# Projecting queries and keys for the next four heads inside the attention loop, one product block per head

## The reference

```python
qkv = x @ W_qkv.T + b_qkv
q, k, v = jnp.split(qkv, 3, axis=-1)          # b, l, 16 heads, 32
scores = jnp.einsum('bqhe,bkhe->bhqk', q, k) * scale
scores = jnp.where(causal[None, None], scores, -jnp.inf)
attn = jax.nn.softmax(scores, axis=-1)
out = jnp.einsum('bhqk,bkhe->bqhe', attn, v)
```

## Time and profile before

| | us |
|---|---|
| median of 3 runs | 1772.81 (1772.62 to 1774.22) |
| the profiled execution's own time | 1772.19 |
| its span in the profile | 1770.0 |
| TensorE busy | 1706.3 (96%) |
| VectorE busy | 1043.6 (59%) |
| ScalarE busy | 736.7 (42%) |
| GpSimd busy | 253.5 (14%) |
| first weights of the projections asked for | at 639.7 |
| first score matmul of the attention | at 784.8 |
| last exponential of the attention | at 1181.5 |

### The profile page before, as it was taken

How to read it: one execution, slowest core, us unless ns; L and a number is a source line. 1 busy time by engine, 2 the same in 40 slices (tenths; PEclk the granted TensorE clock), 3 DMA queues, 4 the chain that set the end, 5 groups by cost and what they waited for, 6 DMA issues and landing times. The chain is left out here.

```text
span 1770.0 us, 24385 instructions
## 1 busy us (share of the span) xinstructions
PE 1706.3 (96%) x8366; PEld 1374.3 (78%) x8366; DVE 1043.6 (59%) x1795; ACT 736.7 (42%) x1528; POOL 253.5 (14%) x247
## 2 busy tenths in 40 slices
PE   6999999999999979979999899999999999999998
PEld 4777878778788868867777677777888888888887
DVE  4322455465424453449999799984565554655776
ACT  4421322232213332239999899982222222222221
POOL 4001200200300030100000000005144031033230
PEclk9999999999999989989999999999999999999999
DMA  7200210110100137833445245505010010011243
GB/s 290 91 13 0 66 42 29 43 48 13 48 7 24 48 111 259 289 152 87 121 138 139 82 132 161 142 27 177 1 48 24 1 48 24 1 48 54 90 131 132
DMA packets 75670, 149.61 MB, mean 85 GB/s; under 512 B 9497, under 2 KB 26521, under 8 KB 74018
## 3 DMA queue, kind: packets, MB, share of 16 engines
q1 hardware_dynamic: 75554, 148.17, 26.9%
HBM read 101.87 MB, written 46.27 MB: 84 GB/s over the span
## 5 line engine op out<-in xcount | busy, mean ns | idle before, releaser
L1509 DVE TENSOR_TENSOR pt_lo<-p_turn,pt_hi 128x512 fp32r<-128x512 f32 (+3 forms) x384 | 201.0, 550 | 25.4 <-ACT pt_hi L1484 17.8
L1502 DVE TENSOR_REDUCE row_top<-p_score 128x1 f32<-128x128 f32 (+7 forms) x256 | 189.5, 750 | 20.9 <-PE p_score L1436 20.6
L1476 ACT ACTIVATE prob<-p_score,row_top 128x128 f32<-128x128 f32 (+7 forms) x256 | 189.8, 744 | 7.9 <-DVE row_top L1502 5.8
L1484 ACT ACTIVATE pt_hi<-p_turn 128x512 fp32r<-128x512 f32 (+3 forms) x384 | 182.0, 493 | 12.7 <-issue 4.9
L1447 PE MATMUL p_turn<-ident,prob 128*128 128x128 f32 x1152 | 183.4, 278 | 3.7 <-DVE pt_lo L1509 3.4
L958 DVE TENSOR_TENSOR hid<-hid,p_up 128x512 f32<-128x512 f32 x64 | 44.0, 688 | 222.3 <-PE p_up L435 206.6
L1845 DVE TENSOR_TENSOR e_hid<-e_hid,e_p_up 128x512 f32<-128x512 f32 x64 | 44.0, 687 | 196.7 <-PE e_p_up L1731 196.7
L1462 PE MATMUL p_o<-pt_hi,v 128*128 128x512 f32 (+3 forms) x384 | 149.2, 396 | 3.9 <-ACT o_both L1492 3.1
L1447 PEld LDWEIGHTS p_turn<-ident,prob 128*128 128x128 f32 x1152 | 133.4, 143 | 17.6 <-DVE pt_lo L1509 4.3
L1434 PE MATMUL p_score<-stack 128*128 128x512 f32 (+3 forms) x384 | 129.8, 393 | 13.9 <-PEq L53 7.0
L705 ACT ACTIVATE hid<-p_gate 128x512 f32<-128x512 f32 x64 | 38.3, 598 | 223.1 <-PE p_gate L435 223.0
(11 more groups left out here) (259 smaller groups left out, 4004.0 us busy)
## 6 DMA issues: line engine op xcount, KB each, us to landing
stack<-qk_parked SPq DMA_DIRECT2D x256, 128.0 KB, 3.9
raw<-in_wgu SPq DMA_DIRECT2D x64, 256.0 KB, 2.8
qk_parked<-qk SPq DMA_DIRECT2D x16, 1024.0 KB, 3.9
v_parked<-v_out SPq DMA_DIRECT2D x16, 512.0 KB, 5.3
v<-v_parked SPq DMA_DIRECT2D x8, 1024.0 KB, 9.4
o_parked<-o_both SPq DMA_DIRECT2D x64, 128.0 KB
res<-in_x SPq DMA_DIRECT2D x8, 512.0 KB
rot<-in_w2t SPq DMA_DIRECT2D x4, 1024.0 KB, 7.4
```

The lines of the kernel that those rows point to most:

```text
L1476: act.activation(prob[r // QB][:, h % 2, r % QB, 0:width_of(r)], p_score[:, r % 2, 0:width_of(r)], ACT.Exp, bias=top[:, r:r + 1], accum_ou ...
L1484: act.activation(pt_hi[:, (BL * h + j) % PT, c0:W], p_turn[:, (BL * h + j) % TB, c0:W], ACT.Copy).then_inc(rounded, 1)
L1502: dve.tensor_reduce(top[:, r:r + 1], p_score[:, r % 2, 0:width_of(r)], AX_X, ALU.max, negate=True).then_inc(topped, 1)
L1509: dve.tensor_tensor(pt_lo[:, slot, c0:W], p_turn[:, (BL * h + j) % TB, c0:W], pt_hi[:, slot, c0:W].bitcast(F32), ALU.subtract).then_inc(sp ...
```

## The change

`project_qkv` becomes `project_first`: it makes quad 0's 8 blocks and the 16 value blocks only. The loops over quads 1 to 3 are gone on all engines, and so is the second half of the values' load, which SP now issues at the start of the attention. SP's order changes too: mask and all 32 loads of the first two stacks come right behind the four stores of quad 0, ahead of the first value store.

The 24 other blocks are made in the attention. Head h of quads 0 to 2 gets the step `job`: four groups of three matmuls on TensorE, a copy on ScalarE, rounding and remainder on VectorE; SP stores every second block, and waits for that store to land before loading the stacks of the next quad. GpSimd splits the next quad's weights in the attention. The block takes a place in the ring of `p_turn`: 13 per head in place of 12, in quad 3 too, where no block is made. The waits that follow from it are in `turn`.

```diff
-                   ("weigh", 5, 0), ("score", 6, 1), ("turn", 11, 0), ("weigh", 6, 0), ("turn", 0, 1),
-                   ("score", 7, 1), ("weigh", 7, 0), ("turn", 1, 1), ("turn", 2, 1), ("weigh", 8, 0),
-                   ("score", 0, 2), ("weigh", 9, 0)],
+                   ("weigh", 5, 0), ("score", 6, 1), ("turn", 11, 0), ("weigh", 6, 0), ("job", 0, 0),
+                   ("turn", 0, 1), ("job", 1, 0), ("score", 7, 1), ("job", 2, 0), ("weigh", 7, 0), ("job", 3, 0),
+                   ("turn", 1, 1), ("weigh", 8, 0), ("score", 0, 2), ("turn", 2, 1), ("weigh", 9, 0)],
...
-                   ("round", 1, 1), ("exp", 7, 1)],
+                   ("job", 0, 0), ("round", 1, 1), ("exp", 7, 1)],
...
-                   ("top", 6, 1), ("rest", 10, 0), ("rest", 11, 0), ("top", 7, 1), ("rest", 0, 1)],
+                   ("top", 6, 1), ("rest", 10, 0), ("rest", 11, 0), ("top", 7, 1), ("rest", 0, 1),
+                   ("job", 0, 0)],
...
+        def slot_of(h, j):
+
+            return ((BL + 1) * h + j) % TB
...
-                wait(pe, split, BL * (HB * it + h) + j - TB + 1)
+                past = j - TB + 1 if j >= TB else (-1 if h and j == 0 else 0)
+                wait(pe, split, BL * (HB * it + h) + past)
+                if h == 0 and j == 1 or h and j == 2:
+                    used = HB * it + h
+                    wait(pe, job_used, min(used, HB * (QUADS - 1)) if isinstance(it, int) else used)
...
+            def job(it, h, k):
+                i, t = divmod(h, 4)
+                if isinstance(it, int) and it == QUADS - 1:
+                    return
+                if k == 0:
+                    if t == 0:
+                        pe.wait_ge(w_split[i], it + 1)
+                    pe.wait_ge(split, BL * (HB * it + h) + BL - TB + 1)
+                acc = p_turn[:, slot_of(h, BL)]
+                pe.matmul(acc, w_hi[:, i, k], x_hi[:, t, k], start=(k == 0), stop=False)
+                pe.matmul(acc, w_hi[:, i, k], x_lo[:, t, k], start=False, stop=False)
+                mm = pe.matmul(acc, w_lo[:, i, k], x_hi[:, t, k], start=False, stop=(k == KD - 1))
+                if k == KD - 1:
+                    mm.then_inc(job_done, 1)
...
+            def job_out(it, h, _):
...
+                act.wait_ge(job_done, HB * it + h + 1)
...
+                wait(act, qk_split, HB * it + h)
+                act.activation(val[:], p_turn[:, slot_of(h, BL)], ACT.Identity, bias=pair_bias[:, h // 4:h // 4 + 1],
+                               scale=scale[:, 0:1]).then_inc(job_used, 1)
...
+                dve.tensor_copy(hi, val[:]).then_inc(qk_rounded, 1)
+                dve.wait_ge(qk_rounded, HB * it + h + 1)
+                dve.tensor_tensor(lo, val[:], hi.bitcast(F32), ALU.subtract).then_inc(qk_split, 1)
...
+                    wait(pool, job_done, HB * (quad - 2) + 4 * i + 4 if quad > 1 else 0)
```

More of the change, by code:

```diff
@@ L1136, in _, with load_w @@
         def _(sp):
[L1137 to L1154, removed]
+            def load_w(i):
+                sp.dma_start(raw_w[:, i], wqk[0, i]).then_inc(w_loaded[i], 16)
+            load_w(0)
+            sp.dma_start(bias[:, 0:2 * QUADS], qk_bias).then_inc(consts, 16)
             sp.dma_start(scale[:], qk_scale).then_inc(consts, 16)
-            load_w(0, 1, True)
+            load_w(1)
             for k in range(KD):
                 sp.dma_start(raw_v[:, k], wv[:, k]).then_inc(wv_loaded, 16)
-            body(0, False)
+            for n in range(4):
+                sp.wait_ge(qk_split, 2 * n + 2)
+                sp.dma_start(qk_dram[2 * (n % 2) + n // 2].rearrange("h p n -> p h n"), qk[:, n % 2].bitcast(F32))\
+                    .then_inc(qk_stored[n % 2], 16)
+            sp.dma_start(mask_f[:], masks).then_inc(mask_loaded, 16)
+            for i in range(2):
+                sp.wait_ge(qk_stored[i], 32)
+            for n in range(2):
+                load_stack(sp, stack, qk_dram, 0, n, first_loaded)
             for m in range(NT):
@@ L1290, in _, with attention @@
             dve.tensor_copy(mask[:], mask_f[:])
-            with dve.Fori(1, QUADS) as it:
-                body(it, False)
-def attention(nc, mask, stack, v, ident, qk_dram, v_dram, o_dram, total, o_both, o_stored, load_next):
+def attention(nc, wqk, x_hi, x_lo, bias, scale, staging, mask, stack, v, ident, qk_dram, v_dram, o_dram, total, o_both, o_stored,
+              load_next):
     G = 2
@@ L1388, in _, with next_weights @@
         def _(sp):
+            def next_weights(quad):
+                for i in range(2):
+                    wait(sp, w_split[i], quad - 1)
+                    sp.dma_start(raw_w[:, i], wqk[quad, i]).then_inc(w_loaded[i], 16)
             def next_stack(it, n):
                 sp.wait_ge(scored, 2 * ROWS * (4 * it + n - 1))
+                wait(sp, qk_stored, 16 * (4 * (it - 1) + 2 * (n % 2) + n // 2 + 1) if it else 0)
                 load_stack(sp, stack, qk_dram, it, n, stacked[n % 2])
@@ L1402, in store_o @@
                     .then_inc(o_stored[(G * h + g) % OS], 16)
-            def body(it, first, last):
+            next_weights(1)
+            load_values(sp, v, v_dram, 0, 1, v_second)
+            for it in range(QUADS):
+                last = it == QUADS - 1
+                if last:
+                    sp.wait_ge(qk_stored, 16 * 4 * (QUADS - 1))
+                    load_next(sp)
                 for h in range(HB):
-                    for g in range(G):
-                        store_o(it, h, g)
+                    store_o(it, h, 0)
+                    if h % 2 and not last:
+                        store_job(it, h // 2)
+                    store_o(it, h, 1)
                     n = h // 2 + 2
@@ L1455, in weigh @@
                     wait(pe, v_loaded[b], 16 * it)
+                    if b == 1 and isinstance(it, int) and it == 0:
+                        pe.wait_ge(v_second, 16)
                 if kb == 0:
```

199 lines of the change are left out of this document (107 added, 92 removed).

## The result

The changed kernel takes 1819.95 us (median of 4 runs, 1819.19 to 1824.16), the kernel before beside it 1773.51 us: a ratio of 1.0265, 95% interval [1.0246, 1.0284]. The forecast was 1820. Ratios here compare undisturbed executions alone; the profiled one of the run e5_narrow_split took 2146 us, so it is left out and none of its rows is read. The profiled execution of the changed kernel took 1819.19 us with a span of 1817.2, against 1772.19 and 1770.0 before. The page's line of busy times says almost nothing about it: TensorE's share went from 96% to 95%.

The account below looks back on a forecast made before the run. Bound: paths through three engines at 93 to 98% of a 12.06 us head. Terms -55.0 + 90.0 + 7.4 + 2.9 + 5.0 = +50.3 us on 1772.2 gave 1822, stated as 1820; 8-in-10 range 1786 to 1834.

Parts of the forecast that it names:

- The removal and SP's queue: Start of attention: 65.7 us earlier without the 24 blocks, less 6.5 stall and 4.2 clock, leaves 55.0 us.
- The stall: Value phase: stack loads ahead delay the first value store, landing in 3.4 us, so TensorE's block 8 waits 6.5 us.
- The clock: TensorE after the gap near 691 us: granted clock of about a half, 4.2 us of work lost.
- Rival 3: Value phase: value stores do not stall TensorE; 10.7 us less, 1809 us; counted within the forecast's 0.58.
- A head with a product block: Seam of two heads: path of 5.94 us, 3.42 more, plus 0.32 on VectorE; 3.74 a head, 90 us for 24.
- The borders: At three borders of four heads turn 1 needs the block's copy finished, some 1 us each; 2.9 us.
- The collisions: Attention: GpSimd's splitting of weights meets VectorE's block split, four meetings of 1.8 us less what is hidden; 5 us.
- The stall in the loop's jump stays: Jump of the attention's loop: its stall remains, as the loops do; no change in time forecast.
- 1: Heads: TensorE alone is the limit, a head grows by 1.9 us, 46 in all; 1763 us, chance 0.10.
- 4: Heads: VectorE leads, its 1.07 us and collisions make a head grow by 4.5 us; 1838 us, chance 0.08.
- 5: Heads: waits of up to 1 us bring the lower clock, adding 34 us; 1854 us, chance 0.03.
- 2: Heads: unseen slack takes 1 to 1.5 us off the path of each of 24; 1784 to 1796 us, chance 0.19.

Follow-up runs that it names:

- e5_narrow_split: Changed kernel with VectorE's rounding and remainder of a product block over 8 of 512 columns in the loop's 16 heads; 1816.63 us, ratio 1.0234 to before.
- e4_last_ring: Changed kernel with 12 places of the ring per head in the last quad; 1812.75 us, ratio 1.0225 to before.
- e10_loads_later: Changed kernel with first weight stack loaded after the sixth value store, second stack and value load at the attention's start; 1808.46 us, ratio 1.0195 to before.
- e2: Changed kernel without the second group of three matmuls of each product block, between turn 0 and score 7; 1804.33 us, ratio 1.0169 to before.
- the new tables: Changed kernel with another order inside heads, split one head later, 12-place last ring, later loads, middle loop written out; 1754.49 us, ratio 0.9886 to before.

## Why the prediction was right, step by step

The time agrees to 0.05 us, which is luck: the sum gave 1822, and the 2 us taken off it as "a few tenths I counted twice" rest on no row; the terms were off by up to 3.4 us each, and most of the errors cancel. What holds up is the mechanism of the large term, the path through a head. The spans rose by 47.2 us: the first maximum of row 7 starts 54.5 us earlier (794.7 before, 740.2 after), the 31 intervals from there on grew by 103.3 (385.5 to 488.8), and what follows the last one is 1.6 us shorter, which nothing here explains.

- **The removal and SP's queue: right in sum.** -55.0 was forecast; the first score matmul came 54.56 us earlier (784.80 to 730.24), inside "729 to 731". The stall was undersized in its cause: a store landed in 6.4 us (692.13 to 698.52), not 3.4, and TensorE lost 7.0 us in the window where I had 6.5. The clock was oversized: granted 0.90 over the 26 us behind the gap, which is 5.2 us at the lower level or 2.6 lost, not "about a half". The value blocks then came every 2.80 us for 2.72, 1.3 us over 16 of them, a term that I did not have. The low clock at the attention's start is in both kernels, but I gave it no term and it lasts longer in this profile: granted 0.50 for 13 us and 0.79 for the next 7, against 0.58 and then 1.00 before. The first interval grew by 3.24 us (11.87 to 15.11) in the change and by 1.92 in e4_last_ring and e10_loads_later, where the low clock was over some 4 us sooner after the attention's start; so some 1.3 us of the change's time is this, and it comes and goes between executions.
- **Where the stall ends: half told.** Rival 3 said 10.7 us less if the stores did not stall TensorE. Taking only the stall away gave 2.0 us, because the second stack and the value load were next in line; with these out too the stretch up to the attention fell by 9.6. "Where a stall goes, say what is late next" was the step I left out.
- **A head with a product block: right.** Forecast path from block 10's split to the end of exponential 7: 5.94 us. In the rows after, with the split of block 10 ending 0.40 us into its row as before, it runs from 785.15 to 791.25, 6.10: turn 0 0.10 later, the two groups of matmuls 0.09 and 0.10 longer, the rest within 0.1 either way and in part shorter. Ordinary heads grew by 3.85 us (12.10 to 15.95 in quad 0, on average), forecast 3.74. The two runs without one group show that it is the path and not the work.
- **Smaller terms.** The last six intervals grew by 7.4 us together, 1.23 each (forecast 7.4 for seven, 1.05 each). The borders cost less than the 1 us each that I gave them: the intervals ahead of two of them are 16.51 us where 16.05 is usual, 0.45 more, and grew by 4.09, 0.24 more than ordinary heads. The collisions cost 2.6 us in the three places that can be sized, not 5: the subtraction is held 0.97 us, and the next copy, which in the projections stood right behind it and cost another 1.1, is not there.
- **"The stall in the loop's jump stays": wrong by 3.4 us.** The interval at the jump is 19.90 us before and 20.40 after, so that head grew by 0.5 and not by 3.9. The stall itself was shorter: ScalarE stood 4.90 us before and 2.26 after, VectorE 3.31 and 1.54 (rows in the last section). So was the low clock behind it, 6.9 us before and 3.4 after, worked out from these stretches, two before and one after:

```profile
996.00:1003.00 7.00, 5.06 (x21) 4.12 (x21) 3.23 (x7) 4.34 (x12) 0.00 (x0) 0.60 0.08 27
1003.00:1010.00 7.00, 6.96 (x43) 5.53 (x42) 6.56 (x11) 5.95 (x14) 0.00 (x0) 0.91 0.05 14
```

```profile
1008.00:1016.00 8.00, 7.96 (x45) 6.33 (x43) 6.37 (x12) 6.44 (x16) 0.00 (x0) 0.79 0.06 20
```

An estimate from these: 2.6 us less stall and 1.7 us less work lost to the clock are enough to offset a block's 3.9, and the block need not have hidden in the stall. In the versions with the loop that interval is 18.9 to 20.4 us, and in the three below 19.2 (e2, e4 and e10) the clock stayed at 1.00. Why the stall was shorter with the change stays open.
- **Rivals.** 1: for this order it falls; its size was about right as a bound, since the new tables reach 2.17 us of growth a head where I had 1.9. 4: refuted by the narrow split. 5: waits of up to 2.1 us on VectorE and 1.0 us on TensorE's loads left the granted clock at 1.00 in the heads away from the jump, so the rule on cycling banks (the Trainium skill, TensorE: Matmul & The Clock Gate, A second HAM failure mode: psum-queue depth-cycling) did not show at gaps of this length. 2 had no slack behind it: ordinary heads grew by 0.1 us more than forecast.

## What to carry to other kernels

Work that runs alone in its own phase costs its length; moved, as here, into a loop in which three engines are locked to each other, it costs its length on the longest path through the seam, and a place where an engine would wait anyway is free (0.68 us of matmuls: 0 or 0.7 us a head, by position alone). So follow one iteration from wait to wait before placing work, put it ahead of the wait and not behind it, and give each consumer of its result a slot where that engine already idles. When a stall is taken out of a phase, read what ends the phase next; and hold a repaired version against a control that has the same unrelated repairs, here worth 9 us of the 19.

## What the runs showed of the hardware

The interval at the loop's jump was 7.7 us longer than usual in the kernel before (19.90 us for 12.2), on engines that wait for nothing that the profile shows. Rows at the jump, ScalarE and VectorE, in the kernel before:

```profile
997.14 0.39 ACT L1484 ACTIVATE pt_hi<-p_turn 128x256 fp32r<-128x256 f32 x1 [4.90 <-issue]
...
994.75 0.56 DVE L1509 TENSOR_TENSOR pt_lo<-p_turn,pt_hi 128x384 fp32r<-128x384 f32 x1 [3.31 <-issue]
```

And in the kernel after:

```profile
1006.80 0.38 ACT L1499 ACTIVATE pt_hi<-p_turn 128x256 fp32r<-128x256 f32 x1 [2.26 <-issue]
...
1005.93 0.56 DVE L1534 TENSOR_TENSOR pt_lo<-p_turn,pt_hi 128x384 fp32r<-128x384 f32 x1 [1.54 <-issue]
```

The stall has a second price: before, the granted clock fell to 0.60 and 0.91 in the two stretches of 7 us behind it, 6.9 us at the lower level, up to 3.4 us of work lost and part of the 7.7. Written out, the long head was gone and the clock stayed at 1.00 there, and the other heads of the loop's two passes fell from 12.09 to 12.52 us to 12.04 to 12.18 as well; together 9.4 us, an interval of [0.9924, 0.9957] in the ratio. That it is the fetch of instructions behind the jump would fit these rows but was not shown. The 2.80 us instead of 2.72 for a value block of the same twelve matmuls (392 to 399 ns each for 389, at a granted clock of 1.00, in the run with the later loads too) stays open.
